# A graph network's adjacency products on one NeuronCore: four packed buffers instead of two, and VectorE closes a chunk two slots later

## What is computed

```python
def step(f, _):                      # layer 2, ten times
    f = f * src_norm[:, None]
    agg = jax.ops.segment_sum(f[src], dst, num_segments=n)
    f = agg * dst_norm[:, None]
    f = (1.0 - ALPHA) * f + ALPHA * feat0
...
x_j = x[src]                         # layer 3
out = jax.ops.segment_sum(x_j, dst, num_segments=x.shape[0])
```

## Time and profile before

| | us |
|---|---|
| median of three runs | 19903.8 |
| lowest, highest | 19867.3, 19942.5 |
| profiled execution | 19936.7 |
| its span, first to last instruction | 19934.9 |
| `propagate`, within that span (from about 8342 us to 13519 us) | some 5180 |

### The profile page before, as it was taken

The page is one execution under the profiler, slowest core; times in us unless marked ns, Lnnn a source line. Parts: engine busy times, 40 slices in busy tenths (PEclk is TensorE's granted clock), DMA queues, the critical chain, the costliest instruction groups (busy, mean ns, idle before and its releaser), DMA issues. The chain is left out here.

```text
span 19934.9 us, 398915 instructions
## 1 busy us (share of the span) xinstructions
PE 14773.5 (74%) x139606; PEld 9691.4 (49%) x139607; DVE 10952.7 (55%) x15417; ACT 5231.4 (26%) x10549; POOL 7485.0 (38%) x8530
## 2 busy tenths in 40 slices
PE   3666666666666666699999999986777777777787
PEld 2555555555555555355555555553444444444444
DVE  6444444444443444354555555446777777777777
ACT  2333333332333333000000000003444444444443
POOL 4343343433443442000000000005666666666665
PEclk8666666666666666699999999998999999999999
DMA  2010000000000000155555555551111111111111
GB/s 71 19 23 19 22 20 21 20 22 20 22 22 20 23 20 23 40 178 171 176 171 174 172 172 177 173 163 38 27 27 27 27 27 27 27 26 27 27 28 27
DMA packets 1144165, 1253.76 MB, mean 63 GB/s; under 512 B 399195, under 2 KB 1111895, under 8 KB 1142455
## 3 DMA queue, kind: packets, MB, share of 16 engines
q1 hardware_dynamic: 932547, 1124.29, 18.7%
q0 software_dynamic: 210496, 113.01, 3.9%
HBM read 1143.04 MB, written 93.60 MB: 62 GB/s over the span
## 5 line engine op out<-in xcount | busy, mean ns | idle before, releaser
L1458 POOL DMA_INDIRECT m_src<-x_after_layer,m_idx x3240 | 3164.0, 977 | 6734.6 <-DMA m_idx<-in_src 5620.8
L180 POOL DMA_INDIRECT l_xin<-in_x,l_idx x3240 | 3076.0, 949 | 4605.8 <-DMA l_idx<-in_src 3416.8
L1206 PE MATMUL p_prod<-a_slot,f_parts 128*32 128x448 fp8e4 x90552 | 4475.0, 360 | 418.2 <-issue 283.6
L1206 PEld LDWEIGHTS p_prod<-a_slot,f_parts 128*32 128x32 bf16 x90552 | 2460.3, 99 | 2370.3 <-issue 608.1
L581 PE MATMUL a_ps<-hot_hi,hot_lo 128*128 128x196 bf16 x6272 | 1645.0, 304 | 2122.3 <-ACT a_image L680 1034.4
L1589 PE MATMUL radial_ps<-radial_w,radial_hidden 128*128 128x384 f32 x6480 | 2621.1, 542 | 706.2 <-DVE m_products L1728 425.3
L749 DVE TENSOR_TENSOR hot_hi<-window_hi,number_ps 128x1568 bf16<-128x1568 f32 x784 | 1401.3, 1787 | 2985.2 <-PE degree_ps L582 1532.7
L1594 PE MATMUL m_visit_ps<-m_products,m_onehot 128*128 128x288 f32 x8420 | 2471.8, 444 | 640.1 <-DVE m_onehot L1695 287.6
L1594 PEld LDWEIGHTS m_visit_ps<-m_products,m_onehot 128*128 128x128 f32 x8420 | 1685.5, 203 | 1455.5 <-issue 842.6
L1589 PEld LDWEIGHTS radial_ps<-radial_w,radial_hidden 128*128 128x128 f32 x6480 | 1228.8, 205 | 1990.3 <-issue 764.2
L680 ACT ACTIVATE a_image<-a_ps 128x392 fp8e4<-128x392 f32 x3136 | 1477.6, 496 | 2691.0 <-PE a_ps L581 1509.3
(11 more groups left out here) (202 smaller groups left out, 12633.2 us busy)
## 6 DMA issues: line engine op xcount, KB each, us to landing
a_nibbles<-multiplicity_digit SPq DMA_DIRECT2D x1085, 784.0 KB, 4.5
edge_w<-in_edge_weight SPq DMA_DIRECT2D x324, 320.0 KB
multiplicity_digit<-a_packed SPq DMA_DIRECT2D x392, 196.0 KB
l_xin<-in_x,l_idx POOLq DMA_INDIRECT x3240
m_src<-x_after_layer,m_idx POOLq DMA_INDIRECT x3240
xt<-in_edge_attr SPq DMA_DIRECT2D x324, 80.0 KB, 2.1
edge_directions<-rel_unit SPq DMA_DIRECT2D x12, 675.0 KB
m_unit<-edge_directions SPq DMA_DIRECT2D x324, 25.0 KB
```

What stands on the lines that cost most here:

```text
L180: pool.indirect_dma_start(k.xin[m][:, j, :], None, k.io["x"], bass.IndirectOffsetOnAxis(k.idx[m][:, j:j + 1], 0)).then_inc(k.gathered[m], 16)
L1206: mm = nc.tensor.matmul(view(prod[m][rows, w, :], 0, [[QW, 2], [1, QW]]), source[:, h * HH + j, r * D:(r + 1) * D], slots[h][:, 2 * w:2 * ...
L1458: pool.indirect_dma_start(src[m][:, j, :], None, k.x3_d, bass.IndirectOffsetOnAxis(idx[m][:, j:j + 1], 0)).then_inc(gathered[m], 16)
```

## The change

It has three parts.

1. **Four packed buffers.** The two buffers become one tile of four, and a load may start when the slot four back has been unpacked. A chunk pair has 14 slots, which is not a multiple of four, so the buffer of a slot depends on whether the pair's number is odd. The addresses come from a register on SyncE and on VectorE (`packed_at`). The counts in TensorE's waits move from 2 to 4 with the semaphore's starting value.
2. **A later close.** VectorE closes a chunk not behind the seventh unpacked slot of the next chunk but two slots later, behind the second slot of the chunk after that. The second chunk of a pair is therefore closed in the next turn of the loop. To allow this, the code of a pass is a first pair without that close, a loop over the other six pairs, and a last close behind the loop. VectorE's code for a pass about doubles.
3. **No stored tenth.** To make room, `x_tenth` goes. The one instruction that filled it goes from the start, and each `new_f` (140 in a run) gets one instruction that computes the chunk's tenth. Two layer norms use `agg` as scratch instead.

```diff
--- before.py
+++ after.py
@@ -1096,6 +1096,14 @@
 
 
 TURN_AFTER = 1
+CLOSE_AFTER = 2
+AHEAD = 4
+
+
+def packed_at(odd, j):
+
+    at = j % AHEAD
+    return (at + 2 * odd if at < 2 else at - 2 * odd) * PW_H
 
 
 def propagate(nc, k, s):
@@ -1106,12 +1114,11 @@
     sb, pb, sem = k.sb, k.pb, k.sem
     passes = STEPS + 1
     slots = [sb(f"a_slot{h}", [P, 4, HH, QW], U8, s) for h in range(HG)]
-    packed = [sb(f"a_nibbles{n}", [P, 4 * PW_H], U8, s) for n in range(2)]
+    packed = sb("a_nibbles", [P, AHEAD * 4 * PW_H], U8, s)
     parts = [sb(f"f_parts{t}", [P, NB, 3 * D], BF16, s) for t in range(2)]
     agg = sb("agg", [P, NB, D], F32, s)
     chunk_f = sb("chunk_f", [P, CB * D], F32, s)
     chunk_zero = sb("chunk_zero", [P, CB * D], F32, s)
-    tenth = sb("x_tenth", [P, NB, D], F32, s)
     norms = sb("norms", [P, NB, 2], F32, s)
     mean, var = sb("mean", [P, NB], F32, s), sb("var", [P, NB], F32, s)
     turned = sb("turned", [P, 2, CW], F32, s)
@@ -1145,17 +1152,18 @@
                 u = sp.alloc_register("pairs_sp")
                 sp.reg_mov(u, 0)
 
-                def load(plane, chunk, n, j):
+                def load(plane, chunk, n, odd, j):
 
                     await_alone(sp, k.passed_sp, a_unpacked, n * SLOTS + (j + 1))
-                    sp.dma_start(view(packed[j % 2][:], 0, [[PW_H, 4], [1, PW_H]]),
+                    sp.dma_start(view(packed[:], packed_at(odd, j) * 4, [[PW_H, 4], [1, PW_H]]),
                                  slot_part(plane, chunk, j % HG)).then_inc(a_loaded[j], 16)
 
                 def load_plane(d):
                     with sp.Fori(0, NCH // 2) as c2:
                         n = sp.snap(u, min_val=0, max_val=passes * DIGITS * NCH)
+                        odd = sp.snap(n % 2, min_val=0, max_val=1)
                         for j in range(SLOTS):
-                            load(k.planes[d], c2 * 2 + j // HG, n, j)
+                            load(k.planes[d], c2 * 2 + j // HG, n, odd, j)
                         sp.reg_add(u, u, 1)
                 with sp.Fori(0, passes):
                     load_plane(0)
@@ -1163,8 +1171,9 @@
                         with sp.If(planes > d):
                             load_plane(d)
                 n = sp.snap(u, min_val=0, max_val=passes * DIGITS * NCH)
+                odd = sp.snap(n % 2, min_val=0, max_val=1)
                 for j in range(HG):
-                    load(k.planes[0], 0, n, j)
+                    load(k.planes[0], 0, n, odd, j)
                 sp.wait_ge(x_ready, 1)
                 sp.dma_start(k.x3_d.rearrange("(b p) f -> p b f", p=P), k.x[:]).then_inc(x_stored, 16)
                 sp.wait_ge(x_stored, 16)
@@ -1195,7 +1204,7 @@
                     for h in range(HG):
                         if p is not None:
                             await_alone(pe, k.passed_pe, parts_ready, p * HG + (h + 1))
-                        await_alone(pe, k.passed_pe, a_unpacked, n * SLOTS + (HG * m + h + 3))
+                        await_alone(pe, k.passed_pe, a_unpacked, n * SLOTS + (HG * m + h + AHEAD + 1))
                         for j in range(HH):
                             for r in range(3):
                                 for w in range(2):
@@ -1258,7 +1267,7 @@
                 u = dve.alloc_register("pairs_dve")
                 dve.reg_mov(u, 0)
                 dve.sem_inc(taken, 3)
-                dve.sem_inc(a_unpacked, 2)
+                dve.sem_inc(a_unpacked, AHEAD)
                 for r in range(STRIPS):
                     nc.vector.tensor_copy(select[r * D:(r + 1) * D, :], k.ident[r * D:(r + 1) * D, r * D:(r + 1) * D])
                 for d in range(DIGITS):
@@ -1277,12 +1286,12 @@
                             tt(frm, frm, to(r), ALU.subtract)
                             dve.drain()
 
-                def unpack(n, j, ahead=0):
+                def unpack(n, odd, j, ahead=0):
 
                     await_alone(dve, k.passed_dve, a_loaded[j], n * 16 + (16 + 16 * ahead))
                     await_alone(dve, k.passed_dve, a_used, n * SLOTS + (SLOTS * ahead + j + 1))
                     words = PW_H // 4
-                    frm = view(packed[j % 2][:].bitcast(I32), 0, [[words, 4], [1, words]])
+                    frm = view(packed[:].bitcast(I32), packed_at(odd, j), [[words, 4], [1, words]])
                     half = lambda i: view(slots[j % HG][:].bitcast(I32), i * words, [[2 * words, 4], [1, words]])
                     ts(half(0), frm, NIBBLES, None, ALU.bitwise_and)
                     ts(half(1), frm, 4, NIBBLES, ALU.logical_shift_right, ALU.bitwise_and).then_inc(a_unpacked, 1)
@@ -1295,19 +1304,36 @@
 
                 def one_pass(finish):
 
+                    def close(n, d, m, c2):
+
+                        add(n, m, c2)
+                        if finish is not None:
+                            with dve.If(planes - d == 1):
+                                finish(c2 * 2 + m)
+                                if finish is not into_x and m == 1:
+                                    dve.drain().then_inc(parts_ready, 1)
+
+                    def pair(d, c2, first):
+
+                        n = dve.snap(u, min_val=0, max_val=passes * DIGITS * NCH)
+                        odd = dve.snap(n % 2, min_val=0, max_val=1)
+                        even = dve.snap((n + 1) % 2, min_val=0, max_val=1)
+                        for m in range(2):
+                            for h in range(HG):
+                                unpack(n, even if m else odd, (1 - m) * HG + h, m)
+                                if h + 1 == CLOSE_AFTER:
+                                    if m == 1:
+                                        close(n, d, 0, c2)
+                                    elif not first:
+                                        close(n - 1, d, 1, c2 - 1)
+                        dve.reg_add(u, u, 1)
+
                     with dve.Fori(0, planes) as d:
-                        with dve.Fori(0, NCH // 2) as c2:
-                            n = dve.snap(u, min_val=0, max_val=passes * DIGITS * NCH)
-                            for m in range(2):
-                                for h in range(HG):
-                                    unpack(n, (1 - m) * HG + h, m)
-                                add(n, m, c2)
-                                if finish is not None:
-                                    with dve.If(planes - d == 1):
-                                        finish(c2 * 2 + m)
-                                        if finish is not into_x and m == 1:
-                                            dve.drain().then_inc(parts_ready, 1)
-                            dve.reg_add(u, u, 1)
+                        pair(d, 0, True)
+                        with dve.Fori(1, NCH // 2) as c2:
+                            pair(d, c2, False)
+                        n = dve.snap(u, min_val=1, max_val=passes * DIGITS * NCH)
+                        close(n - 1, d, 1, NCH // 2 - 1)
 
                 def new_f(c):
 
@@ -1315,9 +1341,9 @@
                     dve.drain()
                     tt(view(agg[:], c * (CB * D), [[D, CB], [1, D]]), view(agg[:], c * (CB * D), [[D, CB], [1, D]]),
                        view(norms[:], c * (2 * CB), [[2, CB], [0, D]]), ALU.mult)
+                    ts(chunk_f[:], view(k.x[:], c * (CB * D), [[1, CB * D]]), ALPHA, None, ALU.mult)
                     dve.drain()
-                    nc.vector.scalar_tensor_tensor(chunk_f[:], part, 1.0 - ALPHA, view(tenth[:], c * (CB * D), [[1, CB * D]]),
-                                                   ALU.mult, ALU.add)
+                    nc.vector.scalar_tensor_tensor(chunk_f[:], part, 1.0 - ALPHA, chunk_f[:], ALU.mult, ALU.add)
                     dve.drain()
                     nc.vector.tensor_copy(part, chunk_zero[:])
 
@@ -1344,24 +1370,23 @@
 
                 norm(1, agg)
                 for h in range(2):
-                    unpack(0, h)
+                    unpack(0, 0, h)
                 ts(norms[:], k.small[:], 1.0, None, ALU.max).then_inc(norm_in, 1)
                 dve.wait_ge(norm_out, 2)
                 nc.vector.reciprocal(norms[:], norms[:])
-                ts(tenth[:], k.x[:], ALPHA, None, ALU.mult)
                 dve.drain()
                 tt(agg[:], k.x[:], of_src, ALU.mult)
                 all_parts()
                 dve.drain().then_inc(parts_ready, HG)
                 for h in range(2, HG):
-                    unpack(0, h)
+                    unpack(0, 0, h)
                 with dve.Fori(0, STEPS // 2 - 1):
                     for odd in range(2):
                         one_pass(next_parts(parts[1 - odd]))
                 one_pass(next_parts(parts[1]))
                 one_pass(into_x)
                 dve.drain()
-                norm(3, tenth)
+                norm(3, agg)
                 nc.vector.tensor_copy(agg[:], k.x[:])
                 all_parts()
                 dve.drain().then_inc(parts_ready, HG)
@@ -1369,7 +1394,7 @@
                 dve.drain()
```

(2 more changed lines are left out.)

## The result

The kernel before takes 19908.2 us (median of six runs, 19867.3 to 19951.3), the changed one 19988.2 (six runs, 19964.4 to 20013.9). The ratio is **1.0037, with a 95% interval from 1.0023 to 1.0051**: slower by 0.37%, 74 us by the ratio and 80 us between the medians. The time is 3 us outside the range of the prediction, which ended at 19985, and it is a loss where no change was forecast.

What follows compares the result with a forecast made beforehand. TensorE's products and its loop branches were taken to bound the passes, not VectorE. 19936.7 less 1.7 plus 0.3, with zero for the branches, gave 19935.3 on the profiled execution, 19902 us against the median; range 19815 to 19985.

Steps and rivals of the forecast that it cites:

- What bounds the kernel: Stage of the passes: TensorE's products at full rate plus 59 loop branches, some 500 us; TensorE never waits for VectorE.
- The tenth: Start and closes: minus 1.7 us on the path; 140 closes get a 0.25 us instruction, plus 0.3 us on the path.
- the addresses: Per slot on SyncE and VectorE: register address instructions cost nothing; 183 us if the cover went.
- the two more buffers: VectorE's load waits: most of the 1308.6 us turn into waits for TensorE's slots; TensorE does not feel it.
- the later close: VectorE's waits for turned sums: most of the 711.9 us go, and nobody was waiting.
- What remains is the branch: TensorE's loop branches: moved loads share DMA with code fetches; taken as zero, within 0.5 us on each of 49 branches.
- The slower rival: At the loop branches: each fetch meets a load, twice; together 132 us, giving 20034; chance 0.10.
- No difference beyond 0.5%: Whole kernel: time the same within about 0.5%, 100 us; chance 0.87, against faster 0.06 and slower 0.07.
- The signs named for right or wrong: VectorE's waits and TensorE's pairs: right if load waits fall and pairs take 67 to 69 us; wrong at 65 or 70.
- The sign of a stage outside the passes moving by more than 10 us: Stages outside the passes: a change of more than 10 us there would show the prediction wrong.

Runs made afterwards that it cites:

- The written-out kernels: TensorE's loop over the six further pairs of a pass written out, in the change (0.9747, 19454 us) and in the kernel before (0.9760, 19463 us).

## Why the prediction was wrong

**What bounds the kernel** was read rightly. TensorE does not wait for VectorE; the list of waits named 20 that were the branch's. The written-out kernels show it. They also bear out the rule of the Trainium skill that the prediction weighed ("Runtime: NRT & Kernel Launch", "Instruction fetch mechanics"), that code is prefetched in sequence and a taken branch out of what is held must wait: written out, the loop showed no stall, though the change so written fetched a new piece every 6.2 us (484 packets on q8 from 9000 to 12000 us).

**The tenth, the addresses, the two more buffers and the later close, seen by VectorE**, came as told. The new instruction takes 0.27 us where 0.25 was taken. The waits fell as forecast, by 1268 and 648 us, and nobody had waited for them.

**The step that failed is the last one**, "What remains is the branch", where the prediction says "I take zero for this term" and bounds it by half a microsecond on each of 49 branches, 25 us. It measured 1.25 us at the 25 loop branches of the first kind, 1.3 at the 20 of the second and 1.6 at the four outer ones, 63 us, and 6 us more in the tenth pass, which the prediction had left out as unmoved. Three things were wrong in it.

- The tenth pass was read as a sample of VectorE in step with TensorE. It was so at three of its five branches only, with pairs of 68.91, 69.15 and 70.47 us. At the other two the load was issued 0.4 us behind the branch, and those pairs took 66.94 and 67.28. The mean of 68.55 us mixes the two; the three in step have a mean of 69.51, close to the 69.70 that the change shows. A mean over a mixture was taken for the value of one of its parts.
- The second pass, 68.05, stood for all passes of its kind, whose mean was 68.43. Against that the three pairs in step are 1.1 us longer, an estimate of 53 us for 49 branches that the trace of before would have given.
- For passes of the first kind it said that more matmuls between the stalls "would eat into the second". They do: the second stall is 2.66 us there against 3.88 in the other kind. But there was little to begin with, 1.01 us in the mean and none over half a microsecond at six of the 25, since the loads lay otherwise. The prediction did not look at what second stall those passes had.

**The slower rival was the right mechanism**: "a load in flight at the branch and another one issued while the next piece of code is asked for", at every branch in the same phase. It was given 0.10 against 0.76, and its full price, 132 us, was twice the real one: the pair of 70.47 us is near the top of what such a branch costs in passes of the second kind (68.9 to 70.6, 69.70 in the mean), and in the first kind, where 23 products stand between the stalls and not 4, pairs take 68.59 in the mean. The argument for it, "four buffers in step with TensorE put a load at every branch in the same phase", is the finding; but one load was already under way at most branches before, and what changed is when it is issued. The argument that outweighed it was the mean of the tenth pass.

**The range** ended at 19985 and the time is 19988. It reached so far up only to take in most of the slower rival; the sum was 19902. No difference beyond 0.5% was given 0.87, and the measured 0.37% lies in it, but it is a difference that the runs can tell from none.

**The signs named for right or wrong** did their work in part: pairs between 67 and 69 us were to confirm the forecast, and 69.70 in every second pass lies over that, though not at the 70 that was to show it wrong. The sign of a stage outside the passes moving by more than 10 us came, 41 us at layer 4, and means nothing: that stage moves as much by itself.

## What to carry to other kernels

An engine that is not the bound still decides when its transfers go out, and smoothing it can put every one of them at the same moment of the bound engine's cycle; ask what stands at that moment before calling a faster helper free. Where the bound engine fetches its own code, keep large loads from being asked for just ahead of the fetch, or write the loop out: here the first was worth 0.8% of the kernel with four buffers, 0.4% against the one with two, and the second 2.4% to 2.5% against before, with either number of buffers. And a stretch that shows the new condition only at times must be split by that condition before its mean is used.

## What the runs showed that was not expected

- A branch with its code fetch takes 3.6 us when no load is in front of it and 4.9 when a load of 784 KB was asked for 0.3 us ahead of it. A load asked for behind the fetch did not lengthen it. With the load ahead, the packet with the first piece of code begins to move at 2.6 us, while most packets of that load move from 0.6 to 3.6; the second piece begins at 7.5, where those of the load behind the branch, from 4.5 on, come to their end. Code so comes behind most or all of a load. Why was not tried; the runs show the order only.
- In the eleventh pass, whose code is written apart, neither kernel has a second stall, though the change has the same two loads there. In the other passes the second stall stands behind 23 products or behind 4, always at the same one. What a load costs at a branch so depends on the place in the code too; no run moved that place. In the row below, of the eleventh pass after the change, the 84 products behind the branch run on, and a pair takes 65.0 us:

```profile
13230.00 5.84 PE L1215 MATMUL p_prod<-a_slot,f_parts 128*32 128x448 fp8e4 x84 [3.83 <-issue]
```

- Each branch back in a loop body of two chunks (1176 products) costs 8.5 to 9.5 us here, twice the first stall of 4 to 4.6 us that the timeline shows. The rest is the second stall, and products at a lower clock. Behind the branch at 8512, where TensorE had stood for 3.98 us, the granted clock from 8516 to 8519 us is 0.62, and the 61 products from 8521.93 take 5.65 us, where they need 2.9 at full speed: mostly 1.2 GHz. From 8512 to 8515, where it last worked ahead of the stall, it was 1.00, the 2.4 GHz level.

```profile
8516.00:8519.00 3.00, 1.50 (x20) 0.75 (x24) 0.00 (x0) 0.00 (x0) 0.00 (x0) 0.62 0.70 193
```

- Layer 4's stage, which nothing touched, took between 6356 and 6448 us in the four profiles shown. A single profile can hide a 66 us effect behind it, as the pair before and after nearly did: their spans are 28 us apart.
